# First stage of a graph-and-experts layer: x transposed as loaded, centred weights, and z in three products of high and low parts

## The chip, the cores and the metric

The kernel runs on one core of one Trainium2 chip, in one launch. The metric is the device time of an execution in microseconds. Engines are called by their names: TensorE (PE in the rows; its loads of weights are PEld), VectorE (DVE), ScalarE (ACT), GpSimd (POOL), SyncE (SP).

## The reference, cut to what matters

One layer of a graph transformer on 6250 rows of 256 numbers. Rows are normalised, a graph convolution and a linear attention are added to them, and a layer of 8 experts, of which each row takes two, follows. The first stage serves the graph convolution:

```python
xn = _layernorm(x, axis=-1)                     # (x - mean) / sqrt(var + 1e-5)
neigh_sum = segment_sum(xn[src], dst, 6250)     # 100000 edges, sorted by dst
neigh_mean = neigh_sum / maximum(deg, 1.0)[:, None]
h = concatenate([xn, neigh_mean], axis=-1)
out = relu(h @ W + b)                           # W is 512 x 256
```

A sum over neighbours and a product with the lower half of W may change places: the kernel first makes z = xn @ W[256:512] for every row and then gathers and adds rows of z. Everything is float32.

## The kernel before, in words

There are 49 tiles of 128 rows (the last has 106), and four stages. In the first stage z is made for all rows and stored in HBM (`z_d`); tables on the edges are made beside it. In the second, GpSimd gathers rows of `z_d` by the edges, 784 indirect transfers of 128 rows, TensorE adds them up by matrices of zeros and ones, and the attention and the splitting of the experts' weights run beside that. In the third, rows are routed to their experts, and in the fourth the experts are computed.

The first stage works on 25 units of two tiles (`LN_UNITS`; the last unit is one tile). There is no planner: every engine has its own program, in the order in which the code is written, and the engines wait for one another by semaphores. What an engine does for unit n, before the change:

- SyncE loads the unit of x (`load_x`, 256 KB, line 476), up to 8 units ahead.
- VectorE takes mean and variance (`stats`, lines 1092 and 1096), and after ScalarE's square root (`unit_sd`, line 767) the reciprocal and the bias (`scales`, lines 1104 and 1106).
- ScalarE writes the normalised rows, one instruction for each tile (`unit_xn`, line 770).
- TensorE turns them with an identity matrix into PSUM, four transposes of 128x128 (`turn_unit`, line 1719).
- ScalarE copies the turned rows from PSUM to SBUF (`unit_xnT`, line 785).
- TensorE multiplies them with the weights (`z_unit`, line 1729): four float32 products of 128x128 by 128x256, each of which the trace shows as two instructions.
- ScalarE (even units, `unit_z`, line 793) or VectorE (odd units, `z_unit`, line 1114) copies z from PSUM, and GpSimd (first nine units, line 651) or SyncE (line 498) stores it.

Three buffers each hold normalised rows, turned rows and z (`LN_BUFS`). A copy of z waits in `z_free` until the store of three units before has landed. In iteration n of its loop VectorE does the statistics of unit n+2, the scales of unit n+1 and the copy of unit n-2; in `ln_step(n)` ScalarE does the root of unit n+1, the rows of unit n, the turned rows of unit n-1, the copy of unit n-3, and from the twelfth step on it also clears a part of the accumulator (`zero_acc`, line 799); TensorE does the transposes of unit n and the products of unit n-1.

VectorE's loop also holds eight pieces of work for the tables on the edges, put after given iterations: `sort_check` (after n = 8, begins in line 1121), `step_tables` (10), `step_counts` (12), `step_columns` (13), `turned_src` (15), `local_dst` (17), `turned_columns` (18) and `turned_dst` (20). Three of them, at 15, 18 and 20, take what TensorE has turned for them one step earlier, behind the products of that step.

GpSimd's first gather (line 699) waits for three tables and, in `z_stored`, for the last store of z.

Of the kernel before, what the change touches and what calls it, by code (L numbers as in the profile page):

```python
# [10 lines left out]
ALU = mybir.AluOpType  # L11
# [96 lines left out]
def build_program(nc, x, src, dst, gnn_W, gnn_b, w_qkv, mem_kv, w_out, b_out, g_out, g_pre,  # L108
                  Wr, br, ln_g, ln_b, W1, b1, W2, b2, out):
    ctx = ExitStack()  # L110
    with ctx:
# [42 lines left out]
        xn = [xn_flat[:, 2 * D * h:2 * D * (h + 1)].rearrange("p (t d) -> p t d", d=D) for h in range(LN_BUFS)]  # L154
        zs_flat = lend("a", 6 * D)
        zs = [zs_flat[:, 2 * D * h:2 * D * (h + 1)].rearrange("p (t d) -> p t d", d=D) for h in range(LN_BUFS)]
        xnT_flat = lend("a", 6 * D)
        xnT = [xnT_flat[:, 2 * D * h:2 * D * (h + 1)].rearrange("p (t d) -> p t d", d=D) for h in range(LN_BUFS)]
# [33 lines left out]
        BUCKETS = NT + 1  # L192
        ones_f, before_f, hot, seen, base, ranks, cum = (S_flat[:, k * P:k * P + n] for k, n in enumerate(
# [139 lines left out]
        def tiny3(*shape):  # L333
# [29 lines left out]
            var_ready ln_sd ln_ready xn_ready xnT_mm xnT_ready z_mm z_ready z_copied  # L363
            sd_ready rstd_ready sel_ready qu_weights
            cmp_ready counts_ready srcf_ready qcol_ready cols_ready steps_in dstf_ready stepT_ready tables_ready
            quads_in s_built p_ready acc_done waits_passed
            xa_norm xaT_mm xa_ready xa_out kv_mm kv_act kv_dve kmaxT km_ready kmaxrowT kmaxrow_ready mk_exp ek_sub ek_exp ctx_mm
# [64 lines left out]

        def z_taken(eng, n):

            if n >= 0:
                eng.wait_ge(s["z_copied"], n // 2 + 1)
            if n >= 1:
                eng.wait_ge(s["z_ready"], (n + 1) // 2)
# [321 lines left out]
        def _(act):  # L760
# [11 lines left out]
            def unit_xn(n):  # L772
                t0, nt = tiles_of(n)
                act.wait_ge(s["ln_ready"], n + 1)
                until(act, s["xnT_mm"], n + 1 - LN_BUFS)
                for tt in range(nt):
                    a = norm_x(xn[n % LN_BUFS][:, tt, :], t0 + tt)
                a.then_inc(s["xn_ready"], 1)

            def unit_xnT(n):  # L780
                nt = tiles_of(n)[1]
                h = n % LN_BUFS
                act.wait_ge(s["xnT_mm"], n + 1)
                until(act, s["z_mm"], n + 1 - LN_BUFS)
                act.activation(xnT[h][:, 0:nt, :], x_bank[h][:, 0:nt * D].rearrange("p (t d) -> p t d", d=D),
                               ACT.Copy).then_inc(s["xnT_ready"], 1)

            def unit_z(n):
                nt = tiles_of(n)[1]
                h = n % LN_BUFS  # L790
                act.wait_ge(s["z_mm"], n + 1)
                z_free(act, n)
                act.activation(zs[h][:, 0:nt, :], z_bank[h][:, 0:nt * D].rearrange("p (t d) -> p t d", d=D),
                               ACT.Copy).then_inc(s["z_copied"], 1)
# [6 lines left out]
            def ln_step(n):  # L801
                if n + 1 < LN_UNITS:
                    unit_sd(n + 1)
                if n < LN_UNITS:
                    unit_xn(n)
                if 1 <= n <= LN_UNITS:
                    unit_xnT(n - 1)
                if n >= 3 and n % 2:
                    unit_z(n - 3)
# [248 lines left out]
        def _(dve):  # L1058
# [7 lines left out]
            dve.memset(x_all[:, NT - 1, :], 0.0).then_inc(s["consts_dve"], 1)  # L1066
            dve.memset(ones_b[:, :], 1.0)
# [18 lines left out]


            def stats(n):
                t0, nt = tiles_of(n)
                dve.wait_ge(x_in[n % X_AHEAD], 16 * (n // X_AHEAD + 1))  # L1090
# [18 lines left out]
            def z_unit(n):  # L1109
                nt = tiles_of(n)[1]  # L1110
                h = n % LN_BUFS
                dve.wait_ge(s["z_mm"], n + 1)
                z_free(dve, n)
                dve.tensor_copy(zs[h][:, 0:nt, :], z_bank[h][:, 0:nt * D].rearrange("p (t d) -> p t d", d=D)).then_inc(s["z_ready"], 1)

# [67 lines left out]
            def tables():  # L1183
# [7 lines left out]
                dve.tensor_copy(ed_f[0:EP, :, 0, :], ed[0:EP, :, 0, :]).then_inc(s["srcf_ready"], 1)  # L1191
# [74 lines left out]
            for n in range(-2, LN_UNITS + 2):  # L1266
                if n + 2 < LN_UNITS:
                    stats(n + 2)
                if 0 <= n + 1 < LN_UNITS:
                    scales(n + 1)  # L1270
                if n >= 2 and n % 2:
                    z_unit(n - 2)
# [834 lines left out]
```

## Time and profile before

| | us |
|---|---|
| median of 3 runs | 1972.28 (1969.89 to 1974.74) |
| the profiled execution | 1967.06 |
| its span, from the first to the last instruction | 1965.4 |
| first stage, up to the first gather | 90.3 |
| gathers, first to last start | 90.3 to 1121.3 |
| mean granted clock of TensorE | 0.893 |

The span has four parts by the clock of the trace: the first stage up to 90.3 us, the gathers, the routing of rows up to about 1280 us and the experts up to the end. A row of a timeline gives the start and the length of one instruction, or of a run of like ones (x8), then engine, line, operation and operands, and in brackets how long the engine had been idle before it and what ended that. TensorE's granted clock is 1.00 at its higher level (2.4 GHz) and 0.50 at its lower (1.2 GHz); a stretch with some of both shows a number between.

### The profile page before, as it was taken

How to read it: one execution, taken by the hardware profiler on the slowest of the kernel's cores; microseconds unless marked ns; L12 is line 12 of the kernel's file. 1: busy time of each engine (PE TensorE's matmuls, PEld its weight loads, DVE VectorE, ACT ScalarE, POOL GpSimd, SP SyncE). 2: the span in 40 equal slices, each digit the busy share in tenths (PEclk: the TensorE clock that was granted, in tenths of full speed). 3: DMA queues.
4: the chain of work that ended last, by engine and by line, in shares of the span. 5: the costliest groups of instructions: out<-in, count | busy, mean ns of one | idle time of the engine just before them, and what ended most of it. 6: DMA issues, size and time to landing. Idle time of an engine off the chain costs nothing. (4 is left out here: it accounts for less than half of the span.)

```text
span 1965.4 us, 32482 instructions
## 1 busy us (share of the span) xinstructions
PE 1592.8 (81%) x8582; PEld 1315.7 (67%) x8583; DVE 1123.4 (57%) x3118; ACT 909.9 (46%) x1979; POOL 1138.3 (58%) x1141
## 2 busy tenths in 40 slices
PE   6766667667777777887777836799999999999997
PEld 5655455555655545465555635689999999999996
DVE  6622222222345466675665667667777777777774
ACT  6611111111214233344443478656666666666664
POOL 3177777777777677777777627753333333333333
PEclk9978888888888899998988955589999999999999
DMA  8344444344347666666777558498888788878885
GB/s 218 116 128 126 109 121 117 114 120 122 112 141 230 207 201 212 201 211 208 224 213 222 142 183 275 166 314 224 219 217 217 218 223 221 216 214 216 218 222 127
DMA packets 188121, 368.81 MB, mean 188 GB/s; under 512 B 33325, under 2 KB 134173, under 8 KB 173657
## 3 DMA queue, kind: packets, MB, share of 16 engines
q0 software_dynamic: 77296, 252.50, 46.2%
q1 hardware_dynamic: 102992, 113.64, 18.2%
q10 hardware_dynamic: 7736, 1.52, 0.4%
q8 instruction: 43, 0.70, 0.2%
q14 instruction: 54, 0.43, 0.1%
HBM read 287.94 MB, written 80.39 MB: 187 GB/s over the span
## 5 line engine op out<-in xcount | busy, mean ns | idle before, releaser
L699 POOL DMA_INDIRECT w2s_lent<-z_d,edge_tabs_lent x784 | 776.3, 990 | 289.2 <-issue 239.0
L1317 DVE TENSOR_TENSOR acc_lent<-acc_lent,bank 128x258 f32 x244 | 102.5, 420 | 477.9 <-PE bank L1816 474.3
L1816 PE MATMUL bank<-w2s_lent,G 128*128 x976 | 282.4, 441 | 111.4 <-POOLq L687 111.4
L1816 PE MATMUL bank<-w2s_lent,S_lent 128*128 x976 | 270.6, 426 | 85.6 <-POOLq L687 84.1
L2026 PE MATMUL bank<-w2s 128*128 128x512 f32 x896 | 330.6, 403 | 2.8 <-DMA w2s<-w_d 2.8
L1816 PEld LDWEIGHTS bank<-w2s_lent,G 128*128 128x128 f32 x976 | 208.8, 220 | 176.9 <-issue 139.6
L1816 PEld LDWEIGHTS bank<-w2s_lent,S_lent 128*128 128x128 f32 x976 | 202.3, 213 | 150.0 <-issue 115.1
L743 POOL DMA_INDIRECT out_dram<-G,acc_lent x112 | 179.7, 1605 | 209.3 <-DVE G L1650 170.5
L1040 ACT ACTIVATE G<-bank,acc_lent 128x256 f32<-128x256 f32 x448 | 188.0, 471 | 195.2 <-PE bank L2007 109.1
L2005 PE MATMUL bank<-w2s,acc 128*128 128x256 f32 x896 | 258.9, 289 | 3.7 <-DVE w2s L1629 3.0
L2006 PE MATMUL bank<-w2s,acc 128*128 128x256 f32 x896 | 253.7, 283 | 0.0
L2007 PE MATMUL bank<-w2s,acc 128*128 128x256 f32 x896 | 253.2, 283 | 0.0
L2027 PE MATMUL bank<-w2s 128*128 128x256 f32 x896 | 252.3, 282 | 0.0
L1621 DVE TENSOR_TENSOR acc<-w1s,acc 128x512 fp32r<-128x512 f32 x224 | 154.7, 691 | 149.8 <-ACT acc L1005 107.9
L894 ACT ACTIVATE w1s<-bank,r 128x256 f32<-128x256 f32 x49 | 23.2, 474 | 367.2 <-PE bank L1833 367.2
L2026 PEld LDWEIGHTS bank<-w2s 128*128 128x128 f32 x896 | 169.3, 189 | 33.7 <-issue 3.2
L727 POOL DMA_DIRECT2D w2s<-w_d x112 | 65.6, 587 | 213.4 <-PE bank L2027 201.2
L2005 PEld LDWEIGHTS bank<-w2s,acc 128*128 128x128 f32 x896 | 170.0, 190 | 12.1 <-issue 4.3
L2006 PEld LDWEIGHTS bank<-w2s,acc 128*128 128x128 f32 x896 | 170.7, 190 | 0.0
L2027 PEld LDWEIGHTS bank<-w2s 128*128 128x128 f32 x896 | 170.3, 190 | 0.0
L2007 PEld LDWEIGHTS bank<-w2s,acc 128*128 128x128 f32 x896 | 170.1, 190 | 0.0
L1671 DVE TENSOR_TENSOR w2s<-G,w2s 128x512 fp32r<-128x512 f32 x224 | 154.1, 688 | 8.3 <-ACT w2s L1050 8.3
(318 smaller groups left out, 2572.0 us busy)
## 6 DMA issues: line engine op xcount, KB each, us to landing
w2s<-w_d POOLq DMA_DIRECT2D x112, 1024.0 KB, 5.6
w_d<-w2s_lent SPq DMA_DIRECT2D x64, 256.0 KB, 3.7
acc_lent<-bucket_d SPq DMA_DIRECT2D x56, 266.0 KB, 2.8
w2s_lent<-z_d,edge_tabs_lent POOLq DMA_INDIRECT x784, 2.9
bu_d<-w2s_lent SPq DMA_DIRECT2D x98, 128.0 KB, 1.9
w2s_lent<-bu_d SPq DMA_DIRECT2D x14, 768.0 KB, 8.2
w1s<-in_L_ffn_W_dram SPq DMA_DIRECT2D x8, 1024.0 KB, 6.6
w2s_lent<-in_L_ffn_W_dram SPq DMA_DIRECT2D x32, 256.0 KB, 5.2
```

The lines of the kernel that those rows point to most:

```text
L699: pool.indirect_dma_start(out=ring_rows[:, row % (RING * QUAD), 0:D], out_offset=None, in_=z_d[:, :], in_offset=bass.IndirectOffsetOnAxis( ...
L743: pool.indirect_dma_start(out=out[:, :], out_offset=bass.IndirectOffsetOnAxis(ap=nid[par][:, j:j + 1], axis=0), in_=ys[par][:, j, :], in_o ...
L1040: g = act.activation(raw[q % 2][:, k * MT:(k + 1) * MT], bank[q % 2][:, k * MT:(k + 1) * MT], ACT.Gelu, bias=b1c[1 - par][:, 2 * q + k:2 * ...
L1317: dve.tensor_tensor(to, to, bank[j % DEPTH][:, 0:ACCW], ALU.add).then_inc(s["acc_done"], 1)
L1621: dve.tensor_tensor(w1lo[:, :, cols].bitcast(F32R), w1_part(e, q), w1hi[:, :, cols], ALU.subtract).then_inc(s["w1_ready"], 1)
L1671: dve.tensor_tensor(hlo[:, cols].bitcast(F32R), raw[q % 2], hhi[:, cols], ALU.subtract).then_inc(s["h_split"], 1)
L1816: m = pe.matmul(bank[j % DEPTH][:, 0:ACCW], S_of[j % DEPTH][:, k, :], rows[:, ds(bases[j], ACCW)], start=(k == 0), stop=(k == QUAD - 1))
L2005: pe.matmul(to, hi, x_hi, start=(k == 0), stop=False)
L2006: pe.matmul(to, hi, x_lo, start=False, stop=False)
L2007: m = pe.matmul(to, lo, x_hi, start=False, stop=(k == DC - 1))
L2026: pe.matmul(to.rearrange("p (s d) -> p s d", s=2), hi, w_both, start=False, stop=(c == HC - 1), skip_group_check=True)
L2027: m = pe.matmul(to[:, 0:D], lo, w_both[:, 0, :], start=False, stop=(c == HC - 1), skip_group_check=True)
```

## The change

Transposes now take x as it was loaded, and the normalisation is taken apart. With the mean of each column of the weights taken out of them (`center_weights`), x @ W' equals (x - mean) @ W, and the factor 1/sd of each row is applied when z is copied out of PSUM. `unit_xn`, 49 instructions, is gone. The column means are a product with a matrix of 1/256, made by TensorE before its first transposes; VectorE subtracts them and splits the weights into a high part (rounded to the type fp32r) and a low part (the rest). ScalarE's copy of the turned rows now writes their high part (line 782 after the change), a new instruction of VectorE, `x_rest` (line 1117), writes the low part, and z is made of three fp32r products for each float32 product before: high by high, high by low, low by high. All of z is copied by ScalarE, a tile at a time with the row's factor (line 792). The order of the iterations stays; `x_rest` of unit n-1 stands at the end of VectorE's iteration n, where every second iteration held a copy of z.

```diff
@@ -151,11 +151,14 @@
         kv_all = w1s[:, 0:NT * KVW].rearrange("p (t w) -> p t w", w=KVW)
 
         xn_flat = lend("a", 6 * D)
-        xn = [xn_flat[:, 2 * D * h:2 * D * (h + 1)].rearrange("p (t d) -> p t d", d=D) for h in range(LN_BUFS)]
         zs_flat = lend("a", 6 * D)
         zs = [zs_flat[:, 2 * D * h:2 * D * (h + 1)].rearrange("p (t d) -> p t d", d=D) for h in range(LN_BUFS)]
-        xnT_flat = lend("a", 6 * D)
-        xnT = [xnT_flat[:, 2 * D * h:2 * D * (h + 1)].rearrange("p (t d) -> p t d", d=D) for h in range(LN_BUFS)]
+        def lend_r(n):
+
+            lend("a", n)
+            return w2s_r[:, taken["a"] - n:taken["a"]]
+        x_hi, x_lo = ([lend_r(2 * D).rearrange("p (t d) -> p t d", d=D) for _ in range(LN_BUFS)] for _ in range(2))
+        wn_hi, wn_lo = (lend_r(DC * D).rearrange("p (c d) -> p c d", c=DC) for _ in range(2))
         w_neigh = lend("a", DC * D).rearrange("p (c d) -> p c d", c=DC)
         ring = w2s[:, RING_AT:RING_END]
         ring_rows = ring.rearrange("p (k w) -> p k w", w=ACCW)
...
@@ -430,12 +434,13 @@
         def tiles_of(n):
             return 2 * n, 1 if n == LN_UNITS - 1 else 2
 
+        def x_loaded(eng, n):
+            eng.wait_ge(x_in[n % X_AHEAD], 16 * (n // X_AHEAD + 1))
+
         def z_taken(eng, n):
 
             if n >= 0:
-                eng.wait_ge(s["z_copied"], n // 2 + 1)
-            if n >= 1:
-                eng.wait_ge(s["z_ready"], (n + 1) // 2)
+                eng.wait_ge(s["z_copied"], n + 1)
 
         def z_free(eng, n):
 
@@ -769,29 +774,23 @@
             def norm_x(to, t):
                 return act.activation(to, x_all[:, t, :], ACT.Identity, scale=rstd[:, t:t + 1], bias=mean_var[:, t, 0:1])
 
-            def unit_xn(n):
-                t0, nt = tiles_of(n)
-                act.wait_ge(s["ln_ready"], n + 1)
-                until(act, s["xnT_mm"], n + 1 - LN_BUFS)
-                for tt in range(nt):
-                    a = norm_x(xn[n % LN_BUFS][:, tt, :], t0 + tt)
-                a.then_inc(s["xn_ready"], 1)
-
             def unit_xnT(n):
                 nt = tiles_of(n)[1]
                 h = n % LN_BUFS
                 act.wait_ge(s["xnT_mm"], n + 1)
                 until(act, s["z_mm"], n + 1 - LN_BUFS)
-                act.activation(xnT[h][:, 0:nt, :], x_bank[h][:, 0:nt * D].rearrange("p (t d) -> p t d", d=D),
-                               ACT.Copy).then_inc(s["xnT_ready"], 1)
+                act.activation(x_hi[h][:, 0:nt, :].bitcast(F32R), x_bank[h][:, 0:nt * D].rearrange("p (t d) -> p t d", d=D),
+                               ACT.Copy).then_inc(s["xhi_ready"], 1)
 
             def unit_z(n):
-                nt = tiles_of(n)[1]
+                t0, nt = tiles_of(n)
                 h = n % LN_BUFS
+                act.wait_ge(s["ln_ready"], n + 1)
                 act.wait_ge(s["z_mm"], n + 1)
                 z_free(act, n)
-                act.activation(zs[h][:, 0:nt, :], z_bank[h][:, 0:nt * D].rearrange("p (t d) -> p t d", d=D),
-                               ACT.Copy).then_inc(s["z_copied"], 1)
+                for tt in range(nt):
+                    a = act.activation(zs[h][:, tt, :], z_bank[h][:, tt * D:(tt + 1) * D], ACT.Copy, scale=rstd[:, t0 + tt:t0 + tt + 1])
+                a.then_inc(s["z_copied"], 1)
 
             def zero_acc(n):
 
@@ -801,12 +800,10 @@
             def ln_step(n):
                 if n + 1 < LN_UNITS:
                     unit_sd(n + 1)
-                if n < LN_UNITS:
-                    unit_xn(n)
                 if 1 <= n <= LN_UNITS:
                     unit_xnT(n - 1)
-                if n >= 3 and n % 2:
-                    unit_z(n - 3)
+                if 2 <= n < LN_UNITS + 2:
+                    unit_z(n - 2)
                 if ZEROS_FIRST <= n < LN_UNITS:
                     a = zero_acc(n)
                     if n == LN_UNITS - 1:
...
@@ -1084,10 +1082,16 @@
                 a = dve.tensor_scalar(pm[32 * k:32 * k + 32], pcol[32 * k:32 * k + 32], -32.0 * k, None, ALU.add)
             L.after(a)
 
+            def center_weights():
+
+                dve.wait_ge(s["neigh_mm"], 1)
+                L.after(dve.tensor_tensor(w_neigh, w_neigh, bank[6][:, 0:D].rearrange("p (o d) -> p o d", o=1).to_broadcast([P, DC, D]),
+                                          ALU.subtract))
+                split(dve, L, wn_hi, wn_lo, w_neigh).then_inc(s["neigh_ready"], 1)
 
             def stats(n):
                 t0, nt = tiles_of(n)
-                dve.wait_ge(x_in[n % X_AHEAD], 16 * (n // X_AHEAD + 1))
+                x_loaded(dve, n)
                 for tt in range(nt):
                     a = dve.bn_stats(bst6[:, 2 * (n % LN_BUFS) + tt, :], x_all[:, t0 + tt, :])
                 L.after(a)
...
@@ -1106,13 +1110,12 @@
                 dve.scalar_tensor_tensor(out=mean, in0=mean, scalar=-1.0, in1=r.rearrange("p (t o) -> p t o", o=1),
                                          op0=ALU.mult, op1=ALU.mult).then_inc(s["ln_ready"], 1)
 
-            def z_unit(n):
+            def x_rest(n):
                 nt = tiles_of(n)[1]
                 h = n % LN_BUFS
-                dve.wait_ge(s["z_mm"], n + 1)
-                z_free(dve, n)
-                dve.tensor_copy(zs[h][:, 0:nt, :], z_bank[h][:, 0:nt * D].rearrange("p (t d) -> p t d", d=D)).then_inc(s["z_ready"], 1)
-
+                dve.wait_ge(s["xhi_ready"], n + 1)
+                dve.tensor_tensor(x_lo[h][:, 0:nt, :].bitcast(F32R), x_bank[h][:, 0:nt * D].rearrange("p (t d) -> p t d", d=D),
+                                  x_hi[h][:, 0:nt, :], ALU.subtract).then_inc(s["xnT_ready"], 1)
 
             def sort_check():
 
...
@@ -1266,10 +1269,12 @@
             for n in range(-2, LN_UNITS + 2):
                 if n + 2 < LN_UNITS:
                     stats(n + 2)
+                if n == -2:
+                    center_weights()
                 if 0 <= n + 1 < LN_UNITS:
                     scales(n + 1)
-                if n >= 2 and n % 2:
-                    z_unit(n - 2)
+                if 1 <= n <= LN_UNITS:
+                    x_rest(n - 1)
                 if n == LN_SORT - 3:
                     sort_check()
                 if n == LN_SORT - 1:
...
@@ -1708,15 +1713,20 @@
         @block.tensor
         def _(pe):
             pe.wait_ge(s["consts_dve"], 2)
+            pe.wait_ge(s["neigh_in"], 16)
+            for c in range(DC):
+                m = pe.matmul(bank[6][:, 0:D], mean_of, w_neigh[:, c, :], start=(c == 0), stop=(c == DC - 1))
+            m.then_inc(s["neigh_mm"], 1)
 
             def turn_unit(n):
                 nt = tiles_of(n)[1]
                 h = n % LN_BUFS
-                pe.wait_ge(s["xn_ready"], n + 1)
+                x_loaded(pe, n)
                 until(pe, s["xnT_ready"], n + 1 - LN_BUFS)
                 for tt in range(nt):
                     for c in range(DC):
-                        m = pe.transpose(x_bank[h][:, tt * D + c * P:tt * D + (c + 1) * P], xn[h][:, tt, c * P:(c + 1) * P], ident[:, :])
+                        m = pe.transpose(x_bank[h][:, tt * D + c * P:tt * D + (c + 1) * P], x_all[:, tiles_of(n)[0] + tt, c * P:(c + 1) * P],
+                                         ident[:, :])
                 m.then_inc(s["xnT_mm"], 1)
 
             def z_unit(n):
@@ -1725,13 +1735,16 @@
                 pe.wait_ge(s["xnT_ready"], n + 1)
                 z_taken(pe, n - LN_BUFS)
                 for tt in range(nt):
+                    to = z_bank[h][:, tt * D:(tt + 1) * D]
                     for c in range(DC):
-                        m = pe.matmul(z_bank[h][:, tt * D:(tt + 1) * D], xnT[h][:, tt, c * P:(c + 1) * P],
-                                      w_neigh[:, c, :], start=(c == 0), stop=(c == DC - 1))
+                        hi, lo = (v[h][:, tt, c * P:(c + 1) * P].bitcast(F32R) for v in (x_hi, x_lo))
+                        pe.matmul(to, hi, wn_hi[:, c, :].bitcast(F32R), start=(c == 0), stop=False)
+                        pe.matmul(to, hi, wn_lo[:, c, :].bitcast(F32R), start=False, stop=False)
+                        m = pe.matmul(to, lo, wn_hi[:, c, :].bitcast(F32R), start=False, stop=(c == DC - 1))
                 m.then_inc(s["z_mm"], 1)
 
             def turn_src():
-                pe.wait_ge(s["srcf_ready"], 1)
+                pe.wait_ge(s["cmp_ready"], 2)
                 pe.wait_ge(s["tables_ready"], 1)
                 for j in range(EJ):
                     m = pe.transpose(bank[6 + j // 4][:, j % 4 * P:j % 4 * P + EP], ed_f[0:EP, j, 0, :], ident[0:EP, 0:EP])
@@ -1756,7 +1769,7 @@
                 if n < LN_UNITS:
                     turn_unit(n)
                 if n == 1:
-                    pe.wait_ge(s["neigh_in"], 16)
+                    pe.wait_ge(s["neigh_ready"], 1)
                 if n >= 1:
                     z_unit(n - 1)
             for n in range(LN_SORT - 1):
```

Not shown: the memset of the matrix of 1/256 (VectorE, 128x128, after the edge pads), names of semaphores, and two semaphores that now share another's counter.

VectorE, the start, before: statistics of units 0 to 2 (bn_stats and bn_aggr of line 1092 and 1096 for two tiles, then the scales).

```order
L1092 BN_STATS small<-w1s 128x6 [waits x_in0,dve_links]
L1092 BN_STATS small<-w1s 128x6
L1096 BN_AGGR mean_var<-small 128x2 [waits dve_links]
L1096 BN_AGGR mean_var<-small 128x2
L1092 BN_STATS small<-w1s 128x6 [waits x_in1]
L1092 BN_STATS small<-w1s 128x6
L1096 BN_AGGR mean_var<-small 128x2 [waits dve_links]
L1096 BN_AGGR mean_var<-small 128x2
L1104 RECIPROCAL small<-small 128x2 [waits ln_sd]
```

The same place after; `w2s_lent` in line 1088 is the weights, lines 460 and 461 are their split.

```order
L1096 BN_STATS small<-w1s 128x6 [waits x_in0,dve_links]
L1096 BN_STATS small<-w1s 128x6
L1100 BN_AGGR mean_var<-small 128x2 [waits dve_links]
L1100 BN_AGGR mean_var<-small 128x2
L1088 TENSOR_TENSOR w2s_lent<-w2s_lent,bank 128x512 [waits neigh_mm]
L460 CAST w2s<-w2s_lent 128x512 [waits dve_links]
L461 TENSOR_TENSOR w2s<-w2s_lent,w2s 128x512 [waits dve_links]
L1096 BN_STATS small<-w1s 128x6 [waits x_in1]
L1096 BN_STATS small<-w1s 128x6
```

Three instructions that wait for TensorE and for one another now stand between the statistics of units 0 and 1.

VectorE, iteration 5, before: statistics of unit 7, scales of unit 6, copy of z of unit 3, which waits for the store of unit 0 (`z_out0`).

```order
L1092 BN_STATS small<-w1s 128x6 [waits x_in7]
L1092 BN_STATS small<-w1s 128x6
L1096 BN_AGGR mean_var<-small 128x2 [waits dve_links]
L1096 BN_AGGR mean_var<-small 128x2
L1104 RECIPROCAL small<-small 128x2 [waits ln_sd]
L1106 SCALAR_TENSOR_TENSOR mean_var<-mean_var,small 128x2 [waits dve_links]
L1114 COPY w2s_lent<-bank 128x512 [waits z_out0,z_mm]
```

The same iteration after.

```order
L1096 BN_STATS small<-w1s 128x6 [waits x_in7]
L1096 BN_STATS small<-w1s 128x6
L1100 BN_AGGR mean_var<-small 128x2 [waits dve_links]
L1100 BN_AGGR mean_var<-small 128x2
L1108 RECIPROCAL small<-small 128x2 [waits ln_sd]
L1110 SCALAR_TENSOR_TENSOR mean_var<-mean_var,small 128x2 [waits dve_links]
L1117 TENSOR_TENSOR w2s<-bank,w2s 128x512 [waits xhi_ready]
```

The copy, in every second iteration before, is replaced by `x_rest` in each; the wait for a store has left VectorE.

ScalarE, after: steps 3 to 5. Line 772 is the root, 782 the high part of the turned rows, 792 the two halves of z.

```order
L772 ACTIVATE small<-mean_var,small 128x2 [waits var_ready]
L782 ACTIVATE w2s<-bank 128x512 [waits xnT_mm]
L792 ACTIVATE w2s_lent<-bank,small 128x256 [waits z_mm,ln_ready]
L792 ACTIVATE w2s_lent<-bank,small 128x256
L772 ACTIVATE small<-mean_var,small 128x2 [waits var_ready]
L782 ACTIVATE w2s<-bank 128x512 [waits z_mm,xnT_mm]
L792 ACTIVATE w2s_lent<-bank,small 128x256 [waits z_mm,ln_ready]
L792 ACTIVATE w2s_lent<-bank,small 128x256
L772 ACTIVATE small<-mean_var,small 128x2 [waits var_ready]
L782 ACTIVATE w2s<-bank 128x512 [waits z_mm,xnT_mm]
L792 ACTIVATE w2s_lent<-bank,small 128x256 [waits z_out0,z_mm,ln_ready]
L792 ACTIVATE w2s_lent<-bank,small 128x256
```

Each step now ends with both halves of a z, which wait for the products; the wait for a store (`z_out0`) stands here, ahead of the next step's root and high part.

## Rows read from the trace of the kernel before

**Rows 1.** The gathers' line: duration in ns, least, median, most; first and last start.
```profile
L699 POOL DMA_INDIRECT w2s_lent<-z_d,edge_tabs_lent x784: 940/946/1862, 90.3 to 1121.3; - x196
```

**Rows 2.** Timeline: last products of the stage, first gather.
```profile
83.84 2.79 PE L1729 MATMUL bank<-w2s_lent 128*128 128x256 f32 x12
...
90.32 1.31 POOL L699 DMA_INDIRECT w2s_lent<-z_d,edge_tabs_lent  x1 [33.54 <-issue]
```

**Rows 3.** One stretch: length; busy PE, PEld, DVE, ACT, POOL; clock; DMA share; GB/s.
```profile
62.30:76.60 14.30, 14.11 (x86) 11.63 (x85) 10.87 (x40) 14.30 (x34) 0.00 (x0) 1.00 0.32 106
```

**Rows 4.** Timeline: VectorE's start, the first store, the stall, first and last table piece.
```profile
5.06 1.96 DVE L1081 TENSOR_SCALAR ident<-iota,small 128x128 f32<-128x128 f32 x1
...
9.95 0.74 DVE L1092 BATCH_NORM_STATS2 small<-w1s 128x6 f32<-128x256 f32 x2
...
11.26 0.75 DVE L1092 BATCH_NORM_STATS2 small<-w1s 128x6 f32<-128x256 f32 x2
...
18.61 0.78 POOL L651 DMA_DIRECT2D z_d<-w2s_lent  x1 [5.91 <-ACT w2s_lent L793]
...
29.38 0.69 DVE L1114 COPY w2s_lent<-bank 128x512 f32<-128x512 f32 x1 [7.13 <-DMA z_d<-w2s_lent]
...
34.53 0.06 DVE L1121 MEMSET S_lent<- 128x3 f32 x1
...
76.59 0.72 DVE L1092 BATCH_NORM_STATS2 small<-w1s 128x6 f32<-128x256 f32 x2
```

**Rows 5.** Timeline: how closely ScalarE's and VectorE's instructions follow one another.
```profile
71.50 0.66 ACT L799 ACTIVATE acc_lent<-small 128x532 f32<-128x532 f32 x1
...
72.22 1.11 ACT L770 ACTIVATE w2s_lent<-w1s,mean_var,small 128x256 f32<-128x256 f32 x2
...
74.40 1.11 ACT L770 ACTIVATE w2s_lent<-w1s,mean_var,small 128x256 f32<-128x256 f32 x2
...
89.53 1.29 DVE L1302 TENSOR_TENSOR G<-iota,edge_tabs_lent 128x512 f32<-128x512 f32 x2
...
1699.77 0.84 ACT L1040 ACTIVATE G<-bank,acc_lent 128x256 f32<-128x256 f32 x2 [0.80 <-PE bank L2007]
```

**Rows 6.** Timeline of TensorE: float32 products of a unit; fp32r products of the experts.
```profile
46.78 3.35 PE L1729 MATMUL bank<-w2s_lent 128*128 128x256 f32 x8
...
71.97 1.89 PE L1729 MATMUL bank<-w2s_lent 128*128 128x256 f32 x8
...
1272.18 0.36 PE L2005 MATMUL bank<-w2s,acc 128*128 128x256 f32 x1 [0.64 <-ACT w2s L1050]
...
1273.57 0.28 PE L2007 MATMUL bank<-w2s,acc 128*128 128x256 f32 x1
...
1286.94 0.41 PE L2005 MATMUL bank<-w2s,acc 128*128 128x256 f32 x1
...
1289.29 0.38 PE L2007 MATMUL bank<-w2s,acc 128*128 128x256 f32 x1
```

**Rows 7.** Groups by form: busy us, mean ns of one; idle before and releaser.
```profile
L1629 DVE TENSOR_TENSOR w2s<-bank,w2s 128x512 fp32r<-128x512 f32 x56 | 38.2, 683 | 0.0
...
L456 DVE TENSOR_TENSOR w2s_lent<-w2s_lent 128x512 fp32r<-128x512 f32 x32 | 22.4, 700 | 1.1
...
L455 DVE CAST w2s_lent<-w2s_lent 128x512 fp32r<-128x512 f32 x32 | 13.8, 432 | 12.9 <-DMA w2s_lent<-in_L_ffn_W_dram 12.9
...
L785 ACT ACTIVATE w2s_lent<-bank 128x512 f32<-128x512 f32 x24 | 14.1, 586 | 2.6 <-PE bank L1719 2.6
```

**Rows 8.** VectorE's waits from 34.5 to 76.6 us: total, times, longest.
```profile
DVE w2s_lent L1249 <- PE bank L1744: 1.2, 1, 1.2
DVE w2s_lent L1114 <- DMA z_d<-w2s_lent: 1.1, 1, 1.1
DVE edge_tabs_lent L1264 <- PE bank L1752: 0.7, 1, 0.7
DVE w2s_lent L1114 <- PE bank L1729: 0.5, 1, 0.5
```

More of the change, by code:

```diff
@@ L192, in build_program @@
         BUCKETS = NT + 1
+        mean_of = S_flat[:, 0:P]
         ones_f, before_f, hot, seen, base, ranks, cum = (S_flat[:, k * P:k * P + n] for k, n in enumerate(
@@ L362, in build_program @@
             unsorted_mm unsorted_ready edges_kept row_in row_hot row_rank row_pos row_out bases_mm edges_in_again
-            var_ready ln_sd ln_ready xn_ready xnT_mm xnT_ready z_mm z_ready z_copied
+            var_ready ln_sd ln_ready neigh_mm neigh_ready xhi_ready xnT_mm xnT_ready z_mm z_copied
             sd_ready rstd_ready sel_ready qu_weights
-            cmp_ready counts_ready srcf_ready qcol_ready cols_ready steps_in dstf_ready stepT_ready tables_ready
+            cmp_ready counts_ready qcol_ready cols_ready steps_in dstf_ready stepT_ready tables_ready
             quads_in s_built p_ready acc_done waits_passed
-            xa_norm xaT_mm xa_ready xa_out kv_mm kv_act kv_dve kmaxT km_ready kmaxrowT kmaxrow_ready mk_exp ek_sub ek_exp ctx_mm
+            xa_norm xaT_mm xa_ready xa_out kv_mm kv_act kv_dve kmaxT km_ready kmaxrow_ready mk_exp ek_sub ek_exp ctx_mm
             ctx_ready ctxT_mm ctxT_ready M2_mm M2_ready
@@ L1066, in _ @@
             dve.memset(x_all[:, NT - 1, :], 0.0).then_inc(s["consts_dve"], 1)
+            dve.memset(mean_of, 1.0 / D)
             dve.memset(ones_b[:, :], 1.0)
@@ L1190, in tables @@
                 a.then_inc(s["cmp_ready"], 1)
-                dve.tensor_copy(ed_f[0:EP, :, 0, :], ed[0:EP, :, 0, :]).then_inc(s["srcf_ready"], 1)
+                dve.tensor_copy(ed_f[0:EP, :, 0, :], ed[0:EP, :, 0, :]).then_inc(s["cmp_ready"], 1)
             def step_counts():
@@ L1370, in _ @@
             dve.tensor_copy(kmaxb, km1.to_broadcast([P, HID])).then_inc(s["km_ready"], 1)
-            dve.wait_ge(s["kmaxrowT"], 1)
+            dve.wait_ge(s["kmaxT"], 2)
             L.after(dve.tensor_copy(kmaxrow, bank[6][:, 0:P]))
@@ L1849, in _ @@
             pe.wait_ge(s["km_ready"], 1)
-            pe.transpose(bank[6][:, 0:P], kmaxb, ident[:, :]).then_inc(s["kmaxrowT"], 1)
+            pe.transpose(bank[6][:, 0:P], kmaxb, ident[:, :]).then_inc(s["kmaxT"], 1)
             follow()
```

## The prediction, made before the changed kernel had run

> **What bounds the kernel now.** I read first what the end hangs on, then the stage that the change touches. The 784 gathers run from 90.3 to 1121.3 us [rows 1], 1.31 us apiece, GpSimd going from one to the next, and routing and experts come behind them. So whatever moves the first gather moves the end by as much; the whole effect of the change is the shift of that one instruction. It starts 3.69 us after the last product of z has ended (83.84 + 2.79 = 86.63) [rows 2]: a copy, a store and its landing, which stay. The question is when that last product ends.
>
> The first stage has three parts, by VectorE's clock [rows 4]. Up to 34.53 it starts and then stalls: the first store of z, issued at 18.61, lands at 29.38 behind loads of x, and VectorE's copy waits 7.13 us for it. From 34.53 to 76.59, 42.06 us, it does twelve units and eight pieces for the edge tables in turn. From 76.59 to 86.63, 10.04 us, the last units run out. In the dense stretch at 62.3 to 76.6 TensorE is busy 14.11 and ScalarE 14.30 of 14.30 us, VectorE 10.87 [rows 3].
>
> **The prices.** A unit's float32 products are 8 instructions in 1.89 us at TensorE's higher level and 3.35 at its lower; twelve fp32r products of the same shape, weights loaded for each as here, take 1272.18 to 1273.57 + 0.28 = 1.67 us, and at the lower level 1286.94 to 1289.29 + 0.38 = 2.73 [rows 6]. TensorE gains 0.2 to 0.6 us a unit.
>
> ScalarE loses two normalising instructions a unit: the step between two of them is 74.40 - 72.22 = 2.18 us, with half of a copy of z every other unit (0.59/2 [rows 7], overlapped to about 0.24) 2.42 a unit. It gains z in halves, nearest a scaled 128x256 out of PSUM, two in 0.84 [rows 5].
>
> VectorE pays. Its unit is 11.26 - 9.95 = 1.31 us [rows 4]. The new subtraction has the form of the experts' row of 0.683 us (PSUM and SBUF in, fp32r out) [rows 7]; such instructions follow each other at 1.29 - 0.68 = 0.61 [rows 5]. So a unit becomes 1.31 + 0.61 = 1.92, where it was 1.31 + 0.61/2. The bounds on the subtraction are 0.43 and 0.70 long (the cast and the subtraction of the weights' split [rows 7]); I take 0.68, whose operands are the same.
>
> There is also a new circle. ScalarE's step ends with a copy of z that waits for products, and only behind it come the next root and the next high part, for which `x_rest` and then the products wait. One round serves every second unit: products 1.67, two halves 0.84, clearing and root 72.22 - 71.50 = 0.72 [rows 5], high part 0.59 [rows 7], low part 0.68: 4.50 for two units. That is 2.25 a unit, above VectorE's 1.92 and below the 2.42 of before. No engine is full in it.
>
> **Start.** The identity ends at 7.02 [rows 4], with the new memset perhaps 7.2. Only then does TensorE make the column means: 4 instructions at 3.35/8 = 0.42, to 8.9. VectorE subtracts (0.69), rounds (0.43) and splits (0.70) the weights, to 11.0 with its links. Statistics of unit 2 follow at 11.0 + 1.31 = 12.3 instead of 9.95. Two more units of statistics (14.9), the first `x_rest` (15.6), products at the lower level (18.4), two halves (19.3): the first store goes out at 19.6, 1.0 later. The stall stays, now on ScalarE, with the next root and high part queued behind it and VectorE waiting for these. The loads ahead are the same, so I let the store land 0.7 later, at 30.1; bounds are 0 and 1.0. By then five units have their products, where before there were six: `x_rest` of a unit now stands behind the statistics of the third unit after it. From 30.1: halves, root and high part 0.84 + 0.2 + 0.59, the low part, 32.3; one round at the lower level without clearing (2.73 + 0.84 + 0.2 + 0.59 + 0.68 = 5.04): `sort_check` at 37.3. **+2.8 us**, between 0 (the unit behind is caught up) and 5 (one more round at the lower level costs 2 x 1.06).
>
> **Middle.** Before, 42.06 us hold twelve units at 1.31 (15.7), six copies at 0.61 (3.7) and waits of 1.2, 1.1, 0.7 and 0.5 [rows 8]; the rest, 19.2, are the table pieces, which stay. After: 12 x 1.92 = 23.0, and 19.2, make 42.2. Three of the pieces wait for TensorE's transposes, which stand behind products that now begin only when `x_rest` is done; before, two such waits cost 1.2 and 0.7, and I take 0.9 for each of three, 2.6. Together 44.8: **+2.8 us**, between +0.1 (no such wait) and +7 (four pieces leave TensorE idle long enough that the products behind run at the lower level, 1.06 each, as the row at 46.78 does [rows 6]).
>
> **Tail.** One unit at VectorE's pace (1.92), one round for two units (4.5), one of which the last unit is a single tile (3.8), six products (1.0): 11.2 against 10.04, **+1.2 us**, between +0.6 (VectorE's pace throughout) and +3.3 (both rounds at the lower level).
>
> Costed at nothing: the normalising instructions that go and the cheaper products, since VectorE and the circle set the pace; without that cover TensorE's saving would be 25 x 0.2 = 5 us. GpSimd's and SyncE's queues keep their order.
>
> **Sum.** 2.8 + 2.8 + 1.2 = 6.8 us. The profiled execution would go from 1967.06 to 1973.9. The median of the runs is 5.2 above it; on that scale 1972.28 + 6.8 = 1979.1, say 1979. The bounds add up to +0.7 and +15.3; with the subtraction at 0.43 in all 15 units after the stall's end that VectorE paces, 3.8 less below, -3.1.
>
> **Rivals.**
>
> *ScalarE's relief decides.* It is the full engine in [rows 3], and a round of 2.25 against 2.42 over the 17 units from the first table piece on is -2.9. If the table pieces fall into VectorE's idle time as now, that holds; and if the first stores land soon, VectorE could be at `sort_check` in 11.0 + 2 x 1.31 + 8 x 1.92 = 29.0 instead of 34.53, of which half is -2.8. Together -5.7: 1966. It decides if the copy of unit 3 waits under 3 us. Against it: the loads ahead of the store are unchanged, and VectorE's own work in the middle already equals the stretch of before. The Trainium skill (Perfetto Trace Analysis, Identifying the Most-Contended Engine) says to find the engine with the highest occupancy and to optimise it first; by that rule ScalarE was rightly relieved and this rival wins. The trace agrees on the occupancy, 14.30 of 14.30, but only for a stretch of 14 us.
>
> *The clock decides.* The circle leaves TensorE idle behind each table piece and in each round. With the lower level in four rounds of the middle and two of the tail the sum grows by 6 x 1.06 = 6.4: +13.2, 1985. For it: the 3.35 us at 46.78, right behind a table piece. Against: 1.00 in [rows 3], where waits were as short as these.
>
> *Only the start costs.* The table pieces' waits stay as they were and the tail is quicker by what the middle loses: +2.8, 1975.
>
> **How the numbers follow.** Forecast 0.50, with its own range +3 to +11 (1975 to 1983); the clock 0.20; only the start 0.20; ScalarE's relief 0.10. A difference below 0.3%, 5.9 us, can't be told from none. Slower by more: three fifths of the forecast and all of the clock, 0.50. Faster by more: 0.08 of the relief's 0.10. Within: the rest, 0.42. The range is 1970 to 1988; it takes in the bounds -3 and +15 and most of the rivals.
>
> **What would show it.** The first gather at 97 us, the last product ending near 93.4; `sort_check` at 37.3 and the last table piece done at 82. `x_rest` at 0.68 us, x25; a unit's twelve products in 1.67 where the clock is 1.00. ScalarE's first long wait is for the store of unit 0, some 5 us up to 30. In the tail VectorE, waiting for ScalarE's high part, shows idle time each round that it does not have now. After 97 us everything stands as before, shifted. I am wrong if VectorE's unit with `x_rest` takes clearly less than 1.92, if the stall is gone, or if the distance from the first gather to the end changes by more than 3 us.

## The result and the profile after

The changed kernel takes 1974.17 us (median of 20 runs, 1970.81 to 1980.34), the one before beside it 1969.42: 4.75 us more by the medians (0.24%); the ratio over the executions is 1.0029, with a 95% interval of 1.002 to 1.0038. That is slower, by a little less than the 0.3% that the prediction took as the bound of what can be told. Medians and differences in this document leave out three executions that ran far longer (2104.72 us of the run with the low part not made, and 2015.51 and 2976.6 of the kernel before).

The gathers first, as in [rows 1] (duration least, median, most; first and last start):

```profile
L704 POOL DMA_INDIRECT w2s_lent<-z_d,edge_tabs_lent x784: 940/946/2187, 94.9 to 1125.6; - x196
```

They start 4.6 us later and last as long (1030.7 us against 1031.0), so up to the last gather the first stage holds the whole difference; what the two profiles show behind it is taken up under "One sign that misled". The timeline of the changed kernel at the places of [rows 2, 4]:

```profile
9.90 0.92 DVE L460 CAST w2s<-w2s_lent 128x512 fp32r<-128x512 f32 x1
...
12.77 0.74 DVE L1096 BATCH_NORM_STATS2 small<-w1s 128x6 f32<-128x256 f32 x2
...
20.34 0.78 POOL L656 DMA_DIRECT2D z_d<-w2s_lent  x1 [7.64 <-ACT w2s_lent L792]
...
29.55 0.84 ACT L792 ACTIVATE w2s_lent<-bank,small 128x256 f32<-128x256 f32 x2 [4.75 <-DMA z_d<-w2s_lent]
...
30.61 0.17 DVE L1108 RECIPROCAL small<-small 128x2 f32<-128x2 f32 x1 [4.02 <-ACT small L772]
...
36.09 0.06 DVE L1124 MEMSET S_lent<- 128x3 f32 x1
...
80.21 0.75 DVE L1096 BATCH_NORM_STATS2 small<-w1s 128x6 f32<-128x256 f32 x2
...
91.50 0.28 PE L1743 MATMUL bank<-w2s 128*128 128x256 f32 x1
...
94.88 1.25 POOL L704 DMA_INDIRECT w2s_lent<-z_d,edge_tabs_lent  x1 [36.60 <-DMA z_d<-w2s_lent]
```

The differences, cut as the prediction cut them: `sort_check` at 36.09 instead of 34.53 (+1.56); from there to the end of the last table piece, where the next statistics start, 44.12 instead of 42.06 (+2.06); from there to the end of the last product (91.50 + 0.28 = 91.78) 11.57 instead of 10.04 (+1.53); and from the last product to the first gather 3.10 instead of 3.69 (-0.59). Together 4.56.

Which engine took the place of which, the busy time of 0 to 95 us shows (columns as in [rows 3]; here, in order, the kernel before and the one after):

```profile
0.00:95.00 95.00, 65.89 (x342) 54.30 (x343) 62.33 (x268) 65.89 (x146) 22.01 (x37) 0.93 0.61 169
```

```profile
0.00:95.00 95.00, 61.97 (x442) 57.02 (x443) 71.39 (x281) 54.30 (x131) 18.36 (x34) 0.94 0.60 164
...
20.00:38.00 18.00, 13.88 (x101) 13.24 (x101) 12.00 (x44) 8.78 (x25) 4.36 (x6) 0.91 0.99 286
...
62.00:80.00 18.00, 15.94 (x135) 14.76 (x134) 14.99 (x48) 13.04 (x32) 0.00 (x0) 1.00 0.26 86
```

ScalarE gave up 11.6 us of work, TensorE 3.9, VectorE took on 9.1, and the stage got longer. (The stretch holds 4.7 us of gathers before the change; counted up to each kernel's own first gather it is 10.7, 3.3 and 9.7.) The group of the new subtraction (busy, mean ns | idle before), and then VectorE's waits from 36 to 80.2 us, which answer to [rows 8]:

```profile
L1117 DVE TENSOR_TENSOR w2s<-bank,w2s 128x512 fp32r<-128x512 f32 x24 | 16.5, 686 | 1.8 <-ACT w2s L782 1.1
```

```profile
DVE w1s L1188 <- issue: 1.6, 1, 1.6
DVE edge_tabs_lent L1267 <- PE bank L1765: 0.8, 1, 0.8
DVE edge_tabs_lent L1244 <- PE bank L1750: 0.6, 1, 0.6
DVE small L1108 <- ACT small L772: 0.5, 1, 0.5
```

VectorE has hardly a gap there. The wait marked "issue" stood before too (1.42), so what it waits for others is 1.8 us in 44. Busy time alone would not have named it: from 62 to 80 us TensorE is busy 15.94 of 18 us, VectorE 14.99. Which of the two sets the pace, an experiment has to say.

### The profile page after: what moved, and what is told of

The parts are those of the page before. It is cut to its first block, busy times and chain, and to the rows that moved or that the text cites. A ratio compares the mean times of both kernels' runs of the same rounds, so it can differ in the third digit from the quotient of the medians.

```text
span 1975.3 us, 32646 instructions
## 1 busy us (share of the span) xinstructions
PE 1579.4 (80%) x8684; PEld 1312.8 (66%) x8685; DVE 1134.5 (57%) x3135; ACT 899.9 (46%) x1966; POOL 1136.9 (58%) x1141
## 4 chain that ended last, share of the span: by engine, by line
PE 36%; POOL 4%; DMA 3%; issue 3%; DVE 2%; ACT 2%; SPq 1%; POOLq 0%; DVEq 0%; ACTq 0%
PE bank L2039 10%; PE bank L2018 5%; PE bank L2019 5%; PE bank L2040 5%; PE bank L2020 5%; POOL bucket_d L718 3%; PE bank L1829 1%; PE bank L1989 1%; DMA xTs<-xnT_d 1%; DMA w2s_lent<-z_d,edge_tabs_lent 1%; PE bank L2029 1%; POOL w2s_lent L704 1%; PE bank L1956 1%; DMA out_dram<-acc_lent 0%; PE bank L1945 0%
## 5 line engine op out<-in xcount | busy, mean ns | idle before, releaser
L1829 PE MATMUL bank<-w2s_lent,S_lent 128*128 x976 | 265.8, 421 | 91.3 <-POOLq L692 89.3
L1829 PEld LDWEIGHTS bank<-w2s_lent,S_lent 128*128 128x128 f32 x976 | 198.0, 208 | 153.2 <-issue 119.8
```

What stands on the lines that cost most here:

```text
L1829: m = pe.matmul(bank[j % DEPTH][:, 0:ACCW], S_of[j % DEPTH][:, k, :], rows[:, ds(bases[j], ACCW)], start=(k == 0), stop=(k == QUAD - 1))
```

## The experiments

Theory: VectorE's low part of x paces the stage; the copies of z, now all on ScalarE ahead of the next root and high part, cost the rest. Rivals: TensorE's twelve products, the work on the weights at the start, or an order on ScalarE that has no part in it. In each run the time of the first gather is read from one profiled execution, beside the median of all; single executions differ by several us behind it. The code shown is cut (`...`).

**Without the low part.** In short (VectorE's call and the third product go, ScalarE's high part releases the products):

```
-                               ACT.Copy).then_inc(s["xhi_ready"], 1)
+                               ACT.Copy).then_inc(s["xnT_ready"], 1)
...
-                if 1 <= n <= LN_UNITS:
-                    x_rest(n - 1)
...
-                        m = pe.matmul(to, lo, wn_hi[:, c, :].bitcast(F32R), start=False, stop=(c == DC - 1))
```

> Left out: VectorE's low part of x (0.61 us from start to start, 25 times) and the third product that uses it; ScalarE's high part goes straight to the products. Theory (the low part sets VectorE's pace from 36 us to 80 us): a unit there falls from 1.90 to 1.31 us, the last table piece starts 5 to 7 us earlier than 78.4, the first gather at 88 to 90 instead of 94.9, the time 1967 to 1969. Rival 1 (ScalarE, whose instructions of a unit with a zero come to about 1.85 us from start to start, would set the same pace): the first gather at 93 to 95, the time 1972 to 1974. Rival 2 (only the start costs): no change in the pace of the units, time within 1 of 1974.

Measured: first gather at 81.79, time 1959.41, ratio to before 0.9945 (0.9925 to 0.9964). It is 13.1 us earlier than in the changed kernel, twice what the theory expected, which had counted the units of the middle alone: the middle is 8.0 shorter (36.09 us), the start 1.6 and what comes behind the last table piece 3.5. Both rivals fall. But the run took two things away at once.

**The low part not made, the products kept.** VectorE's call goes; the third product takes the high part a second time.

```
-                        hi, lo = (v[h][:, tt, c * P:(c + 1) * P].bitcast(F32R) for v in (x_hi, x_lo))
+                        hi = lo = x_hi[h][:, tt, c * P:(c + 1) * P].bitcast(F32R)
```

> As the run without the low part, but the products stay twelve a unit: the third product takes the high part again, and VectorE makes no low part. It tells apart what that run took away together, VectorE's 0.61 us and four products (0.55 us) a unit. Theory (VectorE paces the stage): the first gather at 81.5 to 85 as in that run (81.8), the time 1959 to 1962. Rival (TensorE's products and transposes, some 2.1 us a unit, pace it): the first gather at 88 to 95, the time 1967 to 1974.

Measured: 1959.55 us, ratio 0.9956 (0.9939 to 0.9974). `sort_check`, the end of the last table piece, the first gather, and a stretch of that run:

```profile
35.09 0.06 DVE L1124 MEMSET S_lent<- 128x3 f32 x1
...
71.62 0.75 DVE L1096 BATCH_NORM_STATS2 small<-w1s 128x6 f32<-128x256 f32 x2
...
83.51 1.10 POOL L704 DMA_INDIRECT w2s_lent<-z_d,edge_tabs_lent  x1 [28.71 <-DMA z_d<-w2s_lent]
```

```profile
62.00:80.00 18.00, 17.97 (x151) 16.82 (x149) 10.27 (x40) 16.25 (x41) 0.00 (x0) 1.00 0.35 117
```

Of the 13.1 us VectorE's instruction is 94.88 - 83.51 = 11.4, the four products 1.7. The middle has 7.6 of the 11.4 (36.53 us instead of 44.12), and twelve times the instruction's 0.61 are 7.3: there it costs the time that it takes on VectorE. The start has 1.0 and the rest 2.8; there VectorE waits for ScalarE, and the run doesn't tell that time from the link that also went, from the high part over the low part to the products. With VectorE down from 14.99 to 10.27 busy of 18 us, TensorE is full (17.97): it is the next bound, not the present one. The run also says what the rest of the change is worth, 90.32 - 83.51 = 6.8 us earlier than before. In the first gather, the change is a gain of 6.8 and a price of 11.4.

**Without the centring.** The column means and their subtraction go. ScalarE writes the weights' high part, VectorE only the low part.

```
+            act.activation(wn_hi.bitcast(F32R), w_neigh, ACT.Copy).then_inc(s["neigh_mm"], 1)
...
-                split(dve, L, wn_hi, wn_lo, w_neigh).then_inc(s["neigh_ready"], 1)
+                dve.tensor_tensor(wn_lo.bitcast(F32R), w_neigh, wn_hi, ALU.subtract).then_inc(s["neigh_ready"], 1)
```

> Left out: the means of the weights' columns and their subtraction; ScalarE writes the weights' high part, VectorE only their low part, so that VectorE loses the cast of 0.92, the subtraction of 0.69 and the wait of 0.56 us ahead of the second unit. Theory (the first store lands at 29.5 us whether it starts at 18.6 or 20.3, so the start is swallowed by the wait for it): sort check starts at 35.6 to 36.1, first gather 94.4 to 94.9, time 1973.5 to 1974.5. Rival (the prediction's step, that the weights cost the start what VectorE works on them): sort check at 34.0 to 34.6, first gather 92.5 to 93.5, time 1971.5 to 1972.5.

Measured: first gather 96.59, 1974.29 us, ratio 1.0023 (1.001 to 1.0037). This run tells nothing of the centring: ScalarE's wait for the weights stood ahead of its zeros, and VectorE waited 3.58 us for the root at 13.84. So it was made again, with the cast behind the first root and VectorE's part one iteration later:

> The run without the centring again, with ScalarE's cast of the weights placed behind its zeros and its first root: in the first form ScalarE's wait for the weights held its zeros and the root up by 3.6 us. Left out are the means of the weights' columns and their subtraction. Theory (the first store lands at about 29.5 us whenever it is issued between 18.6 and 21.7): sort check at 35.6 to 36.4, first gather 94.4 to 95.2, time 1973.5 to 1975. Rival (the prediction's step, that VectorE's work on the weights costs the start): sort check at 34.0 to 34.6, first gather 92.5 to 93.5, time 1971.5 to 1972.5.

Measured: 1974.47 us, ratio 1.002 (1.0006 to 1.0034), first gather 95.57. The first store, the copy that waits for it, and `sort_check`:

```profile
18.64 0.78 POOL L656 DMA_DIRECT2D z_d<-w2s_lent  x1 [5.94 <-ACT w2s_lent L792]
...
28.99 0.84 ACT L792 ACTIVATE w2s_lent<-bank,small 128x256 f32<-128x256 f32 x2 [5.50 <-DMA z_d<-w2s_lent]
...
36.48 0.06 DVE L1123 MEMSET S_lent<- 128x3 f32 x1
```

The store goes out 1.7 us earlier than in the changed kernel, as early as before the change, and lands 0.6 earlier; the wait grows from 4.75 to 5.50, and `sort_check` is no earlier. VectorE's work on the weights costs nothing that reaches the end.

**The copy of z one step later.**

```
-                if 2 <= n < LN_UNITS + 2:
-                    unit_z(n - 2)
+                if 3 <= n < LN_UNITS + 3:
+                    unit_z(n - 3)
```

> ScalarE copies the z of unit n-3 instead of n-2 in step n, so that the copies of z stand no longer between the products of a unit and the high part of the unit two further on. Theory (the round of two units, 4.5 us, sets the pace of the last units): VectorE's waits for ScalarE's high part and root at the end (1.92, 1.06 and 1.77 us) fall under 0.6, rounds go from 2.25 to 1.9 us a unit, first gather 93.2 to 94.2, time 1972.5 to 1973.5. Rival (VectorE's own 1.9 us sets it there too, and ScalarE's copies only come later): first gather 94.5 to 95.5, time 1974 to 1975.

Measured: first gather 92.25, 1968.02 us, ratio 1.0 (0.9987 to 1.0012). 2.6 us are won, more than expected, but not where the theory put them all. `sort_check` starts at 34.54, so 1.55 are won at the start: the unit's root and high part no longer queue behind the copy that waits for the store. The middle is no shorter (44.29 us). The rest comes at the tail, where VectorE's waits for ScalarE are 1.06, 1.18 and 0.84 us instead of 1.92, 1.06 and 1.77: shorter, not gone.

**Six buffers for the stores.** The three added ones lie where the normalised x was; four semaphores were merged into others.

```
+ZS_BUFS = 6
...
-                    a = act.activation(zs[h][:, tt, :], z_bank...
+                    a = act.activation(zs[z_buf(n)][:, tt, :], z_bank...
```

> z is copied into six buffers instead of three ahead of its stores (the three more lie where the change freed the buffers of the normalised x); four semaphores are merged into others, nothing else is moved. Theory (the wait of 4.0 to 4.7 us for the first store stands on the path of the stage): ScalarE doesn't wait from 24.8 to 29.5, VectorE's 4.0 us from 26.6 are gone, sort check starts at 32 to 33 instead of 36.1, first gather 91 to 92, time 1970 to 1971.5. Rival (the transfers are the bound until 38 us, the loads of x come late instead): VectorE waits for x from about 30 us, sort check 35 to 36, first gather 94 to 95, time within 1 of 1974.

Measured: `sort_check` at 32.00 (4.1 earlier), first gather 91.69 (3.2 earlier, since the middle takes 0.8 more), 1968.55 us, ratio 1.0001 (0.999 to 1.0013). ScalarE has no wait for a store any more; the rival falls, the loads of x were not the bound.

**The three repairs together**, with ScalarE's zeros of units 12 to 24 moved into steps 3 to 15:

```
-                if ZEROS_FIRST <= n < LN_UNITS:
-                    a = zero_acc(n)
+                if 0 <= n - 3 < LN_UNITS - ZEROS_FIRST:
+                    a = zero_acc(n - 3 + ZEROS_FIRST)
```

> The changed kernel's computation whole, with the six store buffers (first gather 91.7 alone), the copies of z one step later (92.3 alone) and ScalarE's last 13 zeros in steps 3 to 15 instead of 12 to 24. Theory (the first two take different waits away, though both shorten the one around the first store): first gather 88.5 to 90.5, time 1965 to 1968, faster than before by up to 4. Rival (VectorE, busy 71 of the 95 us and waiting for transfers in most of the rest, holds it): first gather 91 to 92, time 1968 to 1969.

Measured: `sort_check` 30.81, first gather 90.05, 1968.33 us, ratio 0.9991 (0.9979 to 1.0003). The first gather is where the theory put it, as early as before the change; the time is not (1965 to 1968 expected), and can't be told from before. It is no version to keep: VectorE is busy 71.79 us of 95 here as it was in the changed kernel (71.39).

**No split at all.** x transposed as loaded, centred weights and ScalarE's scaled copies stay; the products are the float32 ones of before.

```
-                        pe.matmul(to, hi, wn_hi[:, c, :].bitcast(F32R), start=(c == 0), stop=False)
...
+                        m = pe.matmul(to, x_hi[h][:, tt, c * P:(c + 1) * P], w_neigh[:, c, :], start=(c == 0), stop=(c == DC - 1))
```

> x transposed as loaded, centred weights, ScalarE's copies of z with the scale, as changed; but no high and low parts: ScalarE copies the transposed x once, and z is the plain f32 product of before (eight instructions a unit, 1.89 us at the higher clock level, 3.35 at the lower). Theory (the split's price is VectorE's 0.61 us a unit, and TensorE's f32 products cost less than that): VectorE's unit is 1.31, TensorE's about 2.35 at the higher level, first gather 85 to 89, time 1964 to 1967, faster than before. Rival (TensorE takes VectorE's place, with the lower level in its share of the stage): first gather 92 to 97, time 1971 to 1976.

Measured: first gather 86.94, 1965.05 us, ratio 0.9979 (0.9967 to 0.9992): faster than both kernels. TensorE is full from 62 to 80 us:

```profile
62.00:80.00 18.00, 18.00 (x110) 15.40 (x109) 11.35 (x45) 15.07 (x39) 0.00 (x0) 1.00 0.30 102
```

From 20 to 38 us it is busy only 13.18 of 18, ScalarE waiting 6.4 us for the first store. So the six buffers were added, and in a second form the later copies and earlier zeros too:

> The run with f32 products and the six store buffers together. Theory (two separate prices: VectorE's low part, 0.61 us a unit, and the wait for the first store, 6.5 us on VectorE there): the wait is gone, TensorE, idle 4.8 of the 18 us from 20 to 38 in the f32 run, is what is left, first gather 82.5 to 84.5 instead of 86.9, time 1960 to 1963. Rival (TensorE, busy in all of 62 to 80 us in the f32 run, holds the end): first gather 86 to 87, time 1964 to 1966.

> As the run before it in this call, with the copies of z one step later and the last zeros in steps 3 to 15. Theory (TensorE holds the units there, ScalarE's order no longer counts): first gather within 0.7 of that run. Rival (ScalarE's place in the round still costs, as it did 2.6 us with the split): first gather 1.5 to 3 us earlier than in that run.

Measured: with six buffers 1960.68 us, ratio 0.9954 (0.9937 to 0.997), with all three 1961.62, 0.9963 (0.9949 to 0.9976). The first gather and TensorE's stretch behind the old stall, in the first of them:

```profile
80.89 0.95 POOL L721 DMA_INDIRECT w2s_lent<-z_d,edge_tabs_lent  x1 [31.18 <-DMA z_d<-w2s_lent]
```

```profile
20.00:38.00 18.00, 17.32 (x97) 14.95 (x95) 11.24 (x54) 12.77 (x34) 5.71 (x8) 1.00 1.04 303
...
62.00:80.00 18.00, 15.47 (x86) 13.21 (x85) 8.49 (x35) 13.60 (x33) 0.00 (x0) 1.00 0.32 110
```

With six buffers the first gather comes earlier than the 82.5 to 84.5 that the theory gave. ScalarE's stall of 6.4 us was worth 6.05 here, nearly all of it; with the split a stall of 4.75 was worth 3.2, because the start won 4.1 and the middle took 0.8 more. In the second form the first gather comes 1.0 us earlier still (79.90), between what theory and rival expected, and the time doesn't show it. The f32 form with six buffers is the version to keep: 8.2 us under before, 13.5 under the change.

All runs in one table. Shifts are against 90.32, differences against the median of the kernel before beside that run (1968.90 to 1969.42):

| Run | first gather, us | shift | time, us | difference |
|---|---|---|---|---|
| changed kernel | 94.88 | +4.6 | 1974.17 | +4.8 |
| without low part | 81.79 | -8.5 | 1959.41 | -9.6 |
| low part not made | 83.51 | -6.8 | 1959.55 | -9.9 |
| without centring, first form | 96.59 | +6.3 | 1974.29 | +5.3 |
| without centring, second form | 95.57 | +5.3 | 1974.47 | +5.1 |
| copies later | 92.25 | +1.9 | 1968.02 | -1.0 |
| six buffers | 91.69 | +1.4 | 1968.55 | -0.5 |
| three repairs | 90.05 | -0.3 | 1968.33 | -1.1 |
| f32 | 86.94 | -3.4 | 1965.05 | -4.4 |
| f32, six buffers | 80.89 | -9.4 | 1960.68 | -8.2 |
| f32, three repairs | 79.90 | -10.4 | 1961.62 | -7.3 |

## Why the prediction was right, and where it was off

**Bound and direction.** The end follows the first gather in all eleven rows, to 3.1 us; the 95% intervals leave open 2 to 4 us to either side. The sum of +6.8 came out as +4.75 in the medians and +4.56 in the stage. Mechanism and sign were right; the start and the middle were put too high, the tail too low, and the stretch behind the last product, which was to stay, lost 0.59. The forecast of 1979 is 4.8 above the measured 1974.17, and 2.9 of that is its base: the median before was 1972.28 in three executions and is 1969.42 in twenty. By the chances, slower by more than 0.3% stood first with 0.50; what came is the second, within it, with 0.42.

**Start, +2.8, measured +1.56.** The store landed at about 29.5 instead of 30.1, and the round behind it, from the end of a low part at 31.7 to 36.09, took 4.4 us instead of the 5.04 that it would have with all its products at the lower level. TensorE, after 4.12 us of waiting, began it with products of 0.28 us, as at the higher level, and went on with 0.41, as at the lower; the granted clock was 0.63 (columns as in [rows 3]):

```profile
31.84 0.39 PE L1741 MATMUL bank<-w2s 128*128 128x256 f32 x1 [4.12 <-DVE w2s L1117]
...
32.89 0.28 PE L1743 MATMUL bank<-w2s 128*128 128x256 f32 x1
...
33.40 0.41 PE L1743 MATMUL bank<-w2s 128*128 128x256 f32 x1
```

```profile
32.00:36.09 4.09, 4.09 (x24) 4.09 (x25) 3.39 (x15) 1.97 (x5) 1.42 (x2) 0.63 0.99 335
```

The long passage on the weights, with the first store later by it, described what happens (statistics of unit 2 at 12.77 for 12.3, the store out at 20.34 for 19.6) and had no effect: the second run without the centring shows it. What does cost the start is the step that the prediction named beside it, root and high part queued behind the copy that waits: with the copies one step later `sort_check` is back at 34.54.

**Middle, +2.8, measured +2.06.** A unit that follows another takes 1.90, as priced (1.92):

```profile
47.25 0.73 DVE L1096 BATCH_NORM_STATS2 small<-w1s 128x6 f32<-128x256 f32 x2
...
49.15 0.74 DVE L1096 BATCH_NORM_STATS2 small<-w1s 128x6 f32<-128x256 f32 x2
```

The mis-sized term is the waits for TensorE's transposes: two, of 0.57 and 0.77, instead of three of 0.9 (2.6). The third wait there, 0.48, is for ScalarE's root.

**Tail, +1.2, measured +1.53.** It was put too low by 0.3, and the 3.69 us behind the last product became 3.10; why these got shorter was not followed up. The idle time each round that the prediction asked for is there, VectorE waiting for ScalarE:

```profile
85.62 0.16 DVE L1108 RECIPROCAL small<-small 128x1 f32<-128x1 f32 x1 [1.92 <-ACT small L772]
...
87.86 0.69 DVE L1117 TENSOR_TENSOR w2s<-bank,w2s 128x512 fp32r<-128x512 f32 x1 [1.06 <-ACT w2s L782]
...
90.32 0.42 DVE L1117 TENSOR_TENSOR w2s<-bank,w2s 128x256 fp32r<-128x256 f32 x1 [1.77 <-ACT w2s L782]
```

**Costed at nothing.** The prediction had the normalising instructions and the cheaper products hidden by VectorE and the circle. With the low part not made the rest of the change is worth 6.8 us. The cheaper products are 3.4 of them, the difference to the f32 run (86.94 - 83.51), where the prediction gave TensorE 5. The other 3.4 (90.32 - 86.94) are not taken apart: normalising instructions have gone from ScalarE, but VectorE has also lost its copies of z, six of them in the middle (3.7 in the prediction), and no run puts one of the two back alone.

**The rivals.** ScalarE's relief: its 11.6 us are gone and the stage is longer, so no. The rule that it drew on, from the Trainium skill (Perfetto Trace Analysis, Identifying the Most-Contended Engine), is to optimise the engine with the highest occupancy first. The trace agrees that ScalarE had it in [rows 3], but the gain that was to follow didn't come. Work went to VectorE, whose own units and table pieces already filled the middle; after the change it is the busiest engine of the stage (71.39 of 95 us). The clock: 0.94 in 0 to 95 us after, 0.93 before, so no. Only the start: by the total this rival (+2.8) is as near to 4.75 as the forecast is; but the start paid only 1.56, and the middle 2.06, so no.

**One sign that misled.** The prediction would have called itself wrong if the distance from the first gather to the end changed by over 3 us. In the two profiled executions it did, from 1875.1 to 1880.4, all of it behind the last gather. The profiled executions lie at 1967.06 and 1976.96, 2.4 under and 2.8 over their medians, which makes those 5.2; the medians have no such difference. The bound of 3 us was too tight for two single executions: over all the runs' profiles this distance goes from 1870.5 (six buffers) to 1886.9 us (without low part).

## What to carry to other kernels

Relieving the fullest engine helps only as far as the engine that takes its work on has room in the same stretch: count that engine's instructions over the whole stretch, side work between the units included, before the exchange. Judge a change with several parts by leaving out one part at a time, since a gain of 6.8 and a price of 11.4 look like a small loss; and try the removal of a stall again after each change of the bound: six buffers were worth 3.2 us under one bound and 6.05 under the next.

## What the runs showed that I had not expected

- The landing of the first store hardly depends here on its issue: issued at 16.97, 18.64 and 20.34 us in three runs, the copy behind it goes on at 29.20, 28.99 and 29.55. Of 3.4 us between the issues 0.6 at most are left between the landings.
- The cast of the weights to fp32r took 0.92 us at the start, where the same form took 0.43 in [rows 7]; GpSimd was issuing transfers over the whole of it; whether that is the cause no run shows.
- The 784 gathers took between 1022.7 us (six buffers) and 1038.6 (without low part) in single executions with the same gathers, and 1031.0 and 1030.7 in the two compared here. A single profile can't show a change of a few us at the end; the first gather is the better mark, as it stands ahead of the gathers.
